# Who tells that TensorE is done: own increments against the next group's increment, and 13 dense parts in four buffers

## What is computed

```python
x = _layernorm(x + _L0_gnn_ref(x, src, dst, edge_weight, ...))     # weighted sums of neighbours, two products, unit rows
x = _layernorm(x + _L1_gnn_ref(x, edge_index, ...))                # three GIN layers
x = _layernorm(x + _L2_gnn_ref(x, ..., src, dst))                  # graph convolution + mixture of 64 experts, batch norm
x = _layernorm(x + _L3_gnn_ref(x, src, dst, edge_weight, ...))     # weighted sums, one product
# in each GIN layer:
agg = jax.ops.segment_sum(h[src], dst, num_segments=N_NODES)
z = (1.0 + eps) * h + agg
m = jax.nn.relu(z @ W1 + b1) @ W2 + b2
```

## Time and profile before

| | |
|---|---|
| median of 3 runs | 6352.02 us (6336.15 to 6355.04) |
| the profiled execution's own time | 6397.59 us |
| its span, first to last instruction | 6395.8 us |
| TensorE matmuls busy | 5173.0 us, 81% |
| TensorE weight loads busy | 4246.0 us, 66% |
| VectorE / GpSimd / ScalarE busy | 3873.3 / 3694.9 / 1677.2 us |
| mean granted TensorE clock | 0.92 |

### The profile page before, as it was taken

One profiled execution on the slowest core, in us unless ns is written; L12 is line 12 of the kernel. 1 busy time (PEld: TensorE's weight loads), 2 busy tenths in 40 slices (PEclk: granted clock), 3 DMA queues, 4 the chain that ended last, 5 costly groups with the idle time before them and its releaser, 6 DMA issues. The chain is left out here.

```text
span 6395.8 us, 104983 instructions
## 1 busy us (share of the span) xinstructions
PE 5173.0 (81%) x36139; PEld 4246.0 (66%) x36139; DVE 3873.3 (61%) x14138; ACT 1677.2 (26%) x4755; POOL 3694.9 (58%) x3731
## 2 busy tenths in 40 slices
PE   4888886688886888858888779888799955888887
PEld 3767764577775677746777667776688833777775
DVE  5777775367774777746777634445888635444444
ACT  2777774011110111111212200000233312333332
POOL 5565666566665666655666556666234352666665
PEclk8999998799998999989999889999899967899998
DMA  5444444666667666686666766666599942333333
GB/s 147 126 129 127 128 137 137 201 201 201 201 202 228 196 196 200 198 260 182 192 189 194 223 188 184 180 182 171 187 324 323 311 141 74 95 97 97 97 96 89
DMA packets 647058, 1124.59 MB, mean 176 GB/s; under 512 B 127578, under 2 KB 458456, under 8 KB 643804
## 3 DMA queue, kind: packets, MB, share of 16 engines
q0 software_dynamic: 211904, 624.43, 34.7%
q1 hardware_dynamic: 434618, 493.35, 24.1%
HBM read 990.13 MB, written 128.55 MB: 175 GB/s over the span
## 5 line engine op out<-in xcount | busy, mean ns | idle before, releaser
L2288 POOL DMA_INDIRECT ring<-planes,REC x1566 | 1511.3, 965 | 978.9 <-issue 417.3
L2385 PE MATMUL PS<-HH,pick 128*128 128x256 bf16 (+1 forms) x7836 | 1044.1, 278 | 193.7 <-issue 164.5
L2385 PEld LDWEIGHTS PS<-HH,pick 128*128 128x128 bf16 x7836 | 764.9, 99 | 384.2 <-issue 234.7
L2288 POOL DMA_INDIRECT ring<-in_x,REC x555 | 534.8, 964 | 338.4 <-PE PS L2364 157.0
L2288 POOL DMA_INDIRECT ring<-table,REC x498 | 478.3, 960 | 368.3 <-issue 242.0
L2288 POOL DMA_INDIRECT more<-planes,REC x522 | 503.4, 964 | 310.7 <-remote 145.1
L2361 PE MATMUL PS<-ring,pick 128*128 128x256 bf16 (+1 forms) x4698 | 640.9, 280 | 48.4 <-issue 43.5
L2385 PE MATMUL PS<-HH,ring 128*128 128x256 bf16 (+1 forms) x3924 | 551.1, 281 | 128.8 <-issue 96.9
L2364 PE MATMUL PS<-ring,pick 128*128 128x256 f32 x2106 | 582.0, 413 | 63.0 <-DMA ring<-table,REC 23.6
L2706 ACT ACTIVATE TZT<-PS 128x256 f32<-128x256 f32 (+1 forms) x294 | 133.7, 455 | 1662.1 <-remote 1084.7
L2361 PEld LDWEIGHTS PS<-ring,pick 128*128 128x128 bf16 x4698 | 467.3, 100 | 144.7 <-issue 67.7
(11 more groups left out here) (377 smaller groups left out, 9488.4 us busy)
## 6 DMA issues: line engine op xcount, KB each, us to landing
HH<-in_L_gnn_w SPq DMA_DIRECT2D x256, 512.0 KB
pick<-dense_blocks SPq DMA_DIRECT2D x480, 160.0 KB
ring<-dense_blocks SPq DMA_DIRECT2D x240, 160.0 KB
HH<-planes SPq DMA_DIRECT2D x64, 576.0 KB
dense_blocks<-HH SPq DMA_DIRECT2D x20, 1568.0 KB
planes<-pick SPq DMA_DIRECT2D x147, 192.0 KB
ring<-planes,REC POOLq DMA_INDIRECT x1566
table<-HN SPq DMA_DIRECT2D x147, 128.0 KB
```

The source lines that it names most:

```text
L2288: pool.indirect_dma_start(slot_row(k, slot, 0, RP if dense else D), None, planes[k] if dense else tables[k], bass.IndirectOffsetOnAxis(ap= ...
L2385: last = mm(bank(5 + n % 2, w), block, plane(m, t, w), start=t == 0 and m == 0, stop=t == NT - 1 and m == 2, skip_group_check=True)
```

## The change

1. TensorE's own increments `s_dq`, `s_hist` and 12 of 13 of `s_wq` go. Who waited for a dense piece or a histogram now waits for `s_prod`, the increment of the product group of the step in which the last such matmul stands (`step_done(k, g)`). ScalarE's wait for `s_wq` goes altogether.
2. So that the group's increment stands behind it, a histogram is issued ahead of the step's products and no longer behind them.
3. A dense tile is loaded in 13 parts (ten of 4 blocks, 128 KB, and three of 3, 96 KB) into 4 buffers (`QA`) in place of 10 in 3.

```diff
-QN = 10
+QN = 13
+QA = 4
-        AB = [v.bitcast(bf16) for v in (ring[:, SLOTS * HST // 2:SLOTS * HST // 2 + AW], pick[:, AT_AB:AT_AB + AW], pick[:, AT_AB + AW:AT_AB + 2 * AW])]
+        AB = [v.bitcast(bf16) for v in [ring[:, SLOTS * HST // 2:SLOTS * HST // 2 + AW]] +
+              [pick[:, AT_AB + j * AW:AT_AB + (j + 1) * AW] for j in range(QA - 1)]]
+        def step_done(k, g):
+
+            return group(k, g) + 1
...
-                return bank(5 + n % 2, w), s_dq, QN * (n + 1)
+                return bank(5 + n % 2, w), s_prod, step_done(k, quarter_done_at(QN * i + QN - 1))
             if kind == "weighted":
                 v = SUMMED.index((k, q))
-                return bank(sums_bank(v), w), s_wq, NB * (v + 1)
+                return bank(sums_bank(v), w), s_wq, v + 1
...
-                if n >= 3:
-                    sp.wait_ge(s_dq, n - 2)
+                if a >= QA:
+                    sp.wait_ge(s_prod, step_done(k, quarter_done_at(a - QA)))
+                elif k > 1:
+                    sp.wait_ge(s_prod, step_done(k - 1, DSTEPS - 1))
...
-                for q in range(3 if k in DENSE_PASSES else 0):
+                for q in range(QA if k in DENSE_PASSES else 0):
...
-                        for q in range(3, ND * QN):
-                            if quarter_done_at(q - 3) == g:
+                        for q in range(QA, ND * QN):
+                            if quarter_done_at(q - QA) == g:
                                 load_quarter(k, q)
...
                     for m in range(3):
                         w = D + 1 if k == 1 and m == 0 else D
                         last = mm(bank(5 + n % 2, w), block, plane(m, t, w), start=t == 0 and m == 0,
                                   stop=t == NT - 1 and m == 2, skip_group_check=True)
-                    if t == QB[q + 1] - 1:
-                        last.then_inc(s_dq, 1)
...
-                last.then_inc(s_wq, 1)
+                if pos == NB - 1:
+                    last.then_inc(s_wq, 1)
...
-                last.then_inc(s_hist, 1)
...
                     if k in DENSE_PASSES:
                         dense(k, g)
+                    if k == 2 and 5 <= g < 5 + NH:
+                        histogram(g - 5)
                     if g < GROUPS[k]:
                         products(k, g)
...
-                    if k == 2 and 5 <= g < 5 + NH:
-                        histogram(g - 5)
...
                     act.wait_ge(s_bw, f + 1)
-                    if f >= OWN:
-                        act.wait_ge(s_wq, f - OWN + 1)
...
                 if g >= 2:
-                    dve.wait_ge(s_hist, g - 1)
+                    dve.wait_ge(s_prod, step_done(2, g + 3))
```

More of the change, by code:

```diff
@@ L1561, in gnn @@
         s_bwe = sem("weighted_banks_copied")
-        s_wq = sem("weighted_blocks_multiplied")
+        s_wq = sem("weighted_sums_done")
         s_xr = [sem(f"first_outputs{j}_loaded") for j in range(2)]
         s_as = [sem(f"dense_tile{j}_stored") for j in range(2)]
-        s_al = [sem(f"dense_quarter{j}_loaded") for j in range(3)]
-        s_dq = sem("dense_quarters_done")
+        s_al = [sem(f"dense_part{j}_loaded") for j in range(QA)]
         s_rl = [sem(f"plane_rows{j}_loaded") for j in range(3)]
@@ L1589, in gnn @@
         s_oh = sem("source_one_hots_built")
-        s_hist = sem("source_histograms_done")
         s_deg = sem("degrees_made")
@@ L2137, in load_rows @@
                 if r == 0 and k > 1:
-                    sp.wait_ge(s_dq, QN * ND * (k - 1))
+                    sp.wait_ge(s_prod, step_done(k - 1, DSTEPS - 1))
                 if n >= 3:
@@ L2157, in _ @@
                 if k == 3:
-                    sp.wait_ge(s_hist, NH)
+                    sp.wait_ge(s_prod, step_done(2, 4 + NH))
                     for j, (lo, hi) in enumerate(((0, GT), (GT, NT))):
@@ L2375, in dense @@
                     if t == QB[q]:
-                        pe.wait_ge(s_al[quarter % 3], 16 * (quarter // 3 + 1))
+                        pe.wait_ge(s_al[quarter % QA], 16 * (quarter // QA + 1))
                     if i == 0 and t % 3 == 0:
@@ L2381, in dense @@
                         pe.wait_ge(s_rl[r % 3], 16 * (r // 3 + 1))
-                    block = AB[quarter % 3][:, (t - QB[q]) * P:(t - QB[q] + 1) * P]
+                    block = AB[quarter % QA][:, (t - QB[q]) * P:(t - QB[q] + 1) * P]
                     for m in range(3):
@@ L2463, in histogram @@
                 for j in range(HALF):
-                    last = mm(bank(7, NT), OHL[g % 2][:, j, :], OHH[g % 2][:, j, :], start=g == 0 and j == 0,
-                              stop=g == NH - 1 and j == HALF - 1, skip_group_check=True)
-                last.then_inc(s_hist, 1)
+                    mm(bank(7, NT), OHL[g % 2][:, j, :], OHH[g % 2][:, j, :], start=g == 0 and j == 0,
+                       stop=g == NH - 1 and j == HALF - 1, skip_group_check=True)
             def transposes(k, p):
@@ L3181, in background @@
                     if g == DSTEPS:
-                        dve.wait_ge(s_dq, QN * ND * 4)
+                        dve.wait_ge(s_prod, step_done(4, DSTEPS - 1))
                     lane_one_hots(lanes_at(g))
```

8 lines of the change are left out of this document (4 added, 4 removed).

## The result

| | median | runs |
|---|---|---|
| before, beside it | 6339.95 us (6332.08 to 6355.04) | 20 |
| after | 6359.81 us (6346.79 to 6369.84) | 20 |

The ratio is 1.0031, 95% interval [1.0025, 1.0038]: the change costs 20 us, half of what was forecast. The profiled execution after has a span of 6367.2 us, about 7 over its median. That of before had 6395.8, 56 over the longer run's median, so the two profiles must not be subtracted: theirs says 29 us faster where the runs say 20 us slower. What they show is where TensorE waits.

What follows compares the result with a forecast made beforehand. TensorE, busy 81% of the span, was taken to bound the kernel. The terms -10 + 61 - 12 + 1 = +40 us, added to the median of 6352.0 us, gave 6392 us, range 6318 to 6435.

Steps and rivals of the forecast that it cites:

- Increments left out: On TensorE, dropping 1187 increments of dense pieces, histograms and weighted products was taken to give back 0 us.
- Rival B: At TensorE's dense matmuls, removed increments shrink the issue gaps and make the kernel faster, 6318 us; chance 0.18.
- The release moves, the mechanism: SyncE's dense loads, released only after the step's products, come late in short windows and make TensorE wait.
- 112 short windows: Dense loads over four passes, 28 each, whose new part is needed 5 blocks into the next step; 1.48 us if bare.
- The release moves, its price: Late dense loads at TensorE were to cost 50 us in bare windows plus 11 us in the other half.
- bare window: A short dense-load window with no transpose, hidden or layer product in it: 1.48 us against a 2.4 us load.
- windows of 6 and 7 blocks: Dense parts needed 6 or more blocks into the next step: 2.8 us or later, in time but for slow loads.
- What takes some of it back: Shorter TensorE waits ahead of hidden and layer products, -12 us; fewer of today's short load waits, -10 us.
- SyncE's order, histogram, weighted products: Later stores and own rows on SyncE 0, histogram ahead of the products +1 us, dropped weighted-product wait 0.
- The signs: In the changed profile: over 60 dense-load waits, 95 to 110 us; issue near 260 us; four passes about 10 us longer each.
- rival C: TensorE's late-load stalls hide in issue gaps or behind another pace-setter, so no change: 6351 us; chance 0.26.
- A: The forecast case: dense loads late in short windows, 56 to 112 new waits under 1.7 us, 6371 to 6435; chance 0.56.

Runs made afterwards that it cites:

- more_increments: The kernel before with an increment of an unwaited spare semaphore on each of the 10,960 dense matmuls that had none: 6381.40 us, ratio 1.0064.
- own_at_short: The changed kernel with own increments back only at the 112 dense parts whose successor is wanted 5 blocks into the next step: 1.0003, 1.0002, 0.9994 to before.
- before_again: The kernel before, unchanged, run once more for a second profile on the faster chip: 5635.79 us.
- step_release_10x3_b: The kernel before with only SyncE's load wait moved to the step's products; 10 parts, three buffers, all increments kept: 1.0060 (same kernel on the faster chip: 1.0460).
- small_loads_after: The changed kernel with every dense load from the fifth on cut to 128 columns: 6339.87 us, ratio 1.0013 to the kernel before.
- small_loads_before: The kernel before with every dense load from the fourth on cut to 128 columns: 6341.22 us, ratio 1.0008 to the kernel before.
- own_release: The changed kernel with each dense part's own increment back and SyncE waiting for it; 13 parts, four buffers kept: 0.9999 and 1.0013 to the kernel before.
- hist_weighted_only: The kernel before without the 387 histogram and weighted-product increments, histogram ahead of the products, dense pieces untouched: 0.9997 and 0.9999 to the kernel before.

## Why the prediction was right and wrong

**Increments left out: right.** 0 was taken; the runs say 0 to 6 us. Rival B is out. The reason given doesn't hold, though, so in part this is luck: it took that a price paid in a run of matmuls must be seen between two of them. more_increments paid 41 us for its increments, and the same 18 matmuls in a row still stand there with 2.14 us. On this kind of chip recorded starts can't bound such a price.

**The release moves, the mechanism: right.** New waits stand 15 matmuls behind a group of products, the 112 short windows make the loss, and SyncE waits for the products' line.

**The release moves, its price: the step that failed.** "A bare window is missed by 0.9 us", 56 x 0.9 + 56 x 0.2 = 61 us, took a microsecond of waiting for a microsecond of time, and said that issue "stays near 260 us". In its place the trace of P has 187 us of new waits, three times the forecast's 61, and 134 us less of other idle time on TensorE; the time went up by 20 us, and by the own_at_short runs 14 to 16 us of such a loss are the 112 windows'. So two errors stand against each other, and that 40 was no further from 20 is their work and not the sum's. The waits were made too small: at 89 of the 112 short windows, 1.9 us each, where 56 of 0.9 and 56 of 0.2 were counted, and 51 more at windows of 6 and 7 blocks, which were called in time. The release itself comes later than the products' recorded end, by 2.1 us in the timeline above, which the window of 1.48 us left out. And their price was made too large: some 16 us for 169. A recorded wait of TensorE is not lost time here; why not is the next paragraph's inference.

**What fits all of this**, and is shown only by its signs: on P and its like TensorE's results come later than its records say. On Q ScalarE starts on a transpose as it ends. Timeline of before_again on Q, pass 2:

```profile
1941.56 0.42 PE L2479 MATMUL PS<-ident,TZ 128*128 128x128 f32 x2
1942.01 0.38 ACT L2706 ACTIVATE TZT<-PS 128x256 f32<-128x256 f32 x1 [6.06 <-PE PS L2479]
```

On P the same pair of the kernel before, in the same pass:

```profile
2161.87 0.42 PE L2479 MATMUL PS<-ident,TZ 128*128 128x128 f32 x2
2164.55 0.38 ACT L2706 ACTIVATE TZT<-PS 128x256 f32<-128x256 f32 x1 [8.42 <-remote]
...
2175.46 0.41 PE L2479 MATMUL PS<-ident,TZ 128*128 128x128 f32 x2
2178.54 0.38 ACT L2706 ACTIVATE TZT<-PS 128x256 f32<-128x256 f32 x1 [8.38 <-remote]
```

0.03 us against 2.26 and 2.67. Over the 294 copies of L2706, each paired in order with its transposes, the mean from the modelled end of the matmul to the copy is 0.06 us on Q, in every kernel, and on P's kind 2.0 us in before, 1.5 to 1.6 in the changed kernel and 1.4 in step_release_10x3_b.

The traces also have the increments themselves. From the modelled end of a group of products to its increment (`s_prod`, dense passes, medians) it is 0.014 us on Q. On P it is 2.4 us in before and 1.3 in after (7 to 9% of these increments are missing there, and the next one was taken for it). And in the changed kernel it hangs on the waits: over its five traces it is 0.7 to 0.9 us where TensorE had waited for a load within the last 30 matmuls, and 2.1 to 2.3 us where it had no idle time over 0.3 us in the last 60. A message that is merely slow would be as slow behind a wait. In own_at_short, whose load waits are fewer and shorter, the two are alike, 2.8 and 2.7 us.

If the matmuls recorded as started are still being worked off for some 2 us, all rows fall in place: the issue gaps are TensorE's queue at its limit; a load that is late for the record is late for the work only by what exceeds that backlog; the more waits for loads a kernel has, the shorter the backlog and the fewer the issue gaps. It also fits that pass 2 pays: its gaps at short windows are 2.8 us long, over the 2.1 us, and those of the other passes, 1.5 us, are not. By these rows 27 x (2.8 - 2.1) = 19 us would be paid there, an estimate; the runs give 9 to 17. It is a rough one: small_loads_after has gaps of 2.5 us there, which would give 11 us, and its pass 2 is 4 us longer than that of small_loads_before (744.6 against 740.9). And TensorE's work on P would go at 0.83 of its pace on Q (615 against 744 us for pass 1), which neither the recorded starts, 0.11 us apart on both, nor the granted clock shows. That the records lead the work is an inference from these delays; nothing here measures the work itself, and what slows it is open.

**What takes some of it back: right in sign, small in size.** -12 us were given for waits ahead of hidden and layer products; at L2507 and L2492 they fell by 33. The 33 are part of the swap, so they are no gain in time of that size. The -10 for fewer short waits of old isn't there: own_release has nearly none of them left and is no faster (0.9999, 1.0013).

**SyncE's order, histogram, weighted products: right.** 0, +1 and 0 were taken; hist_weighted_only gives -2 and -1 us, each with 5 or 6 us to either side, and own_at_short keeps SyncE's new order at no loss. What the histogram's new place costs in pass 2 together with the moved release isn't shown.

**The signs.** More than 60 waits: 138. Their sum 95 to 110: 241. "Issue" near 260: 185. Passes about 10 us longer each: one of four is. This last was named as the mark of rival C, "the new waits are there, but the passes keep their length", and C also named the mechanism, stalls for loads that fall together with issue gaps; "its 83 to 87% busy and the small waits speak against that" was the sentence that held its chance at 0.26. Busy time of modelled matmuls could not say so (and the windows of the earlier trace rows give 84 to 87%). The same trace held the sign: 300 waits of SyncE for a "remote" releaser, 1400.1 us, at a line whose only releasers are dense matmuls of the same core. On Q the same line has 732 waits, all put down to PE. The forecast read the row as waits "for things further back than for TensorE"; they were for TensorE, whose increments came too late for the profile to name it.

The time lies between A and C, 20 us where they gave 40 and -1, inside the range of 6318 to 6435.

## What to carry to other kernels

Before idle time is priced, look at how soon the waiting engines move once the producer's record ends. Where that is 0.03 us, a new wait on the busiest engine costs its length; where it is 2 us and its waits are called "remote", the engine may well have a backlog, and a new wait then costs only what exceeds it. Test a moved release on more than one chip: the same edit cost 4.6% on one and 0.6% on another. And to save increments, drop them where the next one comes in time, but keep those whose waiter has the shortest window: 112 of 1040 gave back the loss, and even then nothing was gained over the kernel before.

## What the runs showed of the hardware

- Two kinds of chip for one program: 5629 us on Q and 6334 to 6401 us on P, R, S, T and U, with granted clocks of 1.00 against 0.97 in the first dense pass. What sets them apart stays open.
- An increment on each dense matmul costs about 4 ns (more_increments on R, 41 us for 10,960), and the recorded starts don't show it.
- From the modelled end of a group of products to its increment 0.014 us pass at the median on Q, and on P 2.4 us in the kernel before and 1.3 in the changed one.
- A recorded wait of TensorE for loads has no fixed price: the same edit brought 266 us more of them on Q for 257 us of time, and on S, where they sum to 379 us, 38 us of time.
- A dense load of 160 KB takes 3.1 us at the median from its issue to the end of its last packet on the faster chip Q, where the DMA engines are busy 79% in pass 1, and 2.6 us on P, at 68%. On Q the increment that tells of the landing comes 3.5 us after the issue. Cut to 32 KB a load takes 1.7 us on T in the kernel before and 1.5 in the changed one.
